# A two-layer attention kernel: layer 1's weights prepared later, and a new order of the first projection

## The chip, the cores and the metric

The kernel runs on one core of a Trainium2 chip. The metric is the device time of one execution in microseconds (us); each figure is the median of several runs. TensorE is called PE in the rows below, VectorE DVE, ScalarE ACT, GpSimd POOL and SyncE SP.

## The reference, cut to what matters

Four images `x` of 256 channels by 64x64 (4096 positions), all float32, pass through two layers, each with a group norm in front and a residual around it:

```python
# layer 0, per image, N = 4096 positions, xn = groupnorm(x)
f = Wq @ xn + bq            # 32 x N
g = Wk @ xn + bk            # 32 x N
h = Wv @ xn + bv            # 256 x N
beta = softmax(f.T @ g, over the first position axis)
x = x + gamma * (h @ beta)
# layer 1, xn = groupnorm(x)
y = relu(bn1(w1 @ xn + b1))              # 32 x N
packed = products of all pairs of y      # 528 x N
x = x + relu(bn2(w2 @ packed + b2))      # 256 x N
```

## The kernel before

Every float32 operand of a large product is split into a float16 high part and a float16 low part, and three float16 matmuls take the place of one float32 matmul. The 4096 positions of an image are cut into 8 chunks of 512 columns. For one chunk of the normed input, ACT makes the high part `xh` (`high`, L994, two instructions), DVE makes the full float32 value `xn` (`normed`, L587, two instructions) and POOL subtracts them into `xl` (`low`, L865). `xn` has two slots, so making the value of chunk k waits until POOL has used that of k-2. PE then makes queries and keys of the chunk (`queries_keys`, L1208, six matmuls) and its values (`value_pair`, L1221, twice twelve matmuls). Both results are split again: ACT copies the high part out of PSUM (`qk_high` L1003, `value_high` L1007), DVE makes the low part (`qk_low` L608, `value_low` L612). SP spreads queries and keys of a chunk over partitions with five small DMAs (`spread`, L331 to L336); `qk_high` and `qk_low` of chunk c write a buffer that the spread of chunk c-2 must have left. For the softmax a running maximum is needed: a "piece" (`piece`, L1227) is one matmul of scores into one of two PSUM banks `tps`, and DVE reduces it (`piece_max`, L617), which frees the bank. 40 pieces are done before the first attention chunk (the list `EARLY`).

Each engine runs its own list in order, and the lists are written out by hand. The front of the kernel has these parts:

- **Loads.** SP issues eight DMAs for small weights (L311), all counted by the semaphore `w_in`, then eight chunks of image 0 and eight of image 1 (L314). ACT, DVE and PE all wait until all eight weight loads have landed.
- **Set-up.** DVE scales the weights of layer 0 in a chain of small instructions, each waiting for the one before; between them it does the statistics of image 0 (`first_stats`, L431, 16 of them, interleaved by `over_stats`). The mark `scaled_qkv` (after L521) lets PE transpose layer 0's weights (L1169, L1171). DVE then scales the weights of layer 1 (L524 to L544), PE transposes them (L1176 to L1180), ACT copies them out (L967 to L973), and DVE makes their low parts (L548, L549, L566 to L569). Only after that come PE's group means (L1199), `variance` (L470 to L474), POOL's power (L858) and `bias` (L478), which give the norm its scale; ACT's first `high` waits for that.
- **Projection of image 0** (`project` on PE, ACT and DVE). ACT and DVE norm four chunks ahead (`RING` = 4); DVE then does seven small instructions of layer 1's scales (L594 to L600), for which ACT waits. After that all three engines follow the list `PARTS`, with the number of pieces after each part in `PIECES`.
- **Attention of image 0** (`attend(0)`): 8 chunks J of 32 steps t. A step is one score matmul (L1243), eight matmuls with the exponential's high part (L1377, L1378), one piece (L1227) and four with its low part (L1384) on PE; two exponentials on ACT (L1017, L1018); one reduction (L617) and one subtraction (L636) on DVE. From image 1 on, layer 1 of the image before runs between the steps. All pieces from here on use the bank `tps[0]`; `tps[1]` serves everything else.

Of the kernel before, what the change touches and what calls it, by code (L numbers as in the profile page):

```python
# [14 lines left out]
MID = 32  # L15
# [31 lines left out]
def build(nc, x, wq, wk, wv, w1, w2, vec, ident, gmean, sel, out):  # L47
# [5 lines left out]
    with ctx:  # L53
# [65 lines left out]
        wqn, wkn, w1n = ot[:, 0], ot[:, 1], ot[:, 2]  # L119
# [28 lines left out]
        w_in = sem("w_in")  # L148
# [53 lines left out]
        NLOADS = 8  # L202
# [28 lines left out]
        JOB = {job: i for i, job in enumerate(JOBS)}  # L231

# [43 lines left out]
        def rows_of(grp):  # L276
            return P if grp < 4 else 96


        PARTS = (("qk", 0), ("qk", 1), ("qk", 2), ("qk", 3), ("v", 0, 0), ("arrived", 0), ("v", 0, 1), ("v", 1, 0),  # L280
# [3 lines left out]
        PIECES = {("arrived", 0): 2, ("v", 0, 1): 2, ("v", 1, 0): 2, ("v", 1, 1): 2, ("qk", 4): 2, ("v", 2, 0): 2,  # L284
# [23 lines left out]
        def _(sp):  # L308
            for dst, src in ((vs[:], vec), (wqn, wq), (wkn, wk), (wvn, wv), (w1n, w1), (w2n, w2), (idn[:], ident),
                             (gm[:], gmean)):  # L310
                sp.dma_start(dst, src).then_inc(w_in, 16)  # L311

# [3 lines left out]
            def pass_through(kind, b, c):  # L316
                k = VISIT[kind, b, c]
                if k:
                    last = THROUGH[k - 1]
                    if last[0] == "stats":  # L320
                        sp.wait_ge(xt_free, (last[1] - 1) * NCH + last[2] + 1)
                    else:
                        sp.wait_ge(xh_ok, JOB[last] + 1)
                        sp.wait_ge(xn_ok, JOB[last] + 1)
                sp.dma_start(xt[:], xv[b, :, :, c * CH:(c + 1) * CH]).then_inc(xt_in, 16)
# [81 lines left out]
        def _(dve):  # L407
# [95 lines left out]
            dve.wait_ge(set_pool, 3)  # L503
# [20 lines left out]
            over_stats(V.tensor_reduce(col(K_MX, 2), w2n, AX, ALU.max, apply_absolute_value=True))  # L524
            over_stats(V.tensor_scalar(col(K_MX, 2), col(K_MX, 2), TINY, 2.0 ** -14, ALU.add, ALU.mult))
            over_stats(V.reciprocal(col(K_U, 2), col(K_MX, 2)))
            for h in range(H2):
                over_stats(V.tensor_scalar(w2n[:, h], w2n[:, h], col(K_U + h), None, ALU.mult))
            over_stats(V.tensor_reduce(col(K_RS1), w1n, AX, ALU.add, apply_absolute_value=True))
            over_stats(V.tensor_tensor(col(K_INV1), vc(V_G1), col(K_W), ALU.mult))  # L530
            over_stats(V.tensor_tensor(col(K_YB), col(K_RS1), col(K_INV1), ALU.mult))
            over_stats(V.tensor_scalar(col(K_RS1), col(K_RS1), TINY, 2.0 ** -7, ALU.add, ALU.mult))
            over_stats(V.reciprocal(col(K_U), col(K_RS1)))
            over_stats(V.tensor_scalar(w1n, w1n, col(K_U), None, ALU.mult))
            mark["scaled"] = s.n

            over_stats(V.tensor_tensor(col(K_T1), vc(V_B1), vc(V_M1), ALU.subtract))
            over_stats(V.scalar_tensor_tensor(col(K_T1), col(K_T1), col(K_INV1), vc(V_BE1), ALU.mult, ALU.add))

            magnitude(col(K_T), col(K_YB), 0.0, over_stats)  # L540
            over_stats(V.tensor_scalar(col(K_YB), col(K_T), GN_MAX, None, ALU.mult))
            magnitude(col(K_U), col(K_T1), 1e-15, over_stats)
            over_stats(V.tensor_tensor(col(K_YB), col(K_YB), col(K_U), ALU.add))
            over_stats(V.tensor_tensor(col(K_YB), col(K_YB), col(K_YB), ALU.mult))  # L544
            mark["squares"] = s.n

            dve.wait_ge(set_act, 1)
            V.tensor_tensor(wqkT[:, 1], acc[0][:, 0:256].rearrange("p (h c) -> p h c", h=2), wqkT[:, 0], ALU.subtract)  # L548
            over_stats(V.tensor_tensor(wvT[:, 1], acc[2][:].rearrange("p (h c) -> p h c", h=2), wvT[:, 0], ALU.subtract))  # L549
            mark["weights_qkv"] = s.n  # L550
# [3 lines left out]
            dve.wait_ge(set_pe, 4)  # L554
            over_stats(V.tensor_scalar(col(K_T), tps[1][:, 8:9], 1.0 / F16_TOP, None, ALU.mult))
            over_stats(V.reciprocal(col(K_A2), col(K_T)))
            mark["square"] = s.n

            over_stats(V.tensor_tensor(col(K_INV2, 2), vc(V_G2, 2), col(K_W + 1, 2), ALU.mult))
            over_stats(V.tensor_tensor(t2[:], vc(V_B2, 2), vc(V_M2, 2), ALU.subtract))  # L560
            over_stats(V.tensor_tensor(t2[:], t2[:], col(K_INV2, 2), ALU.mult))
            over_stats(V.tensor_tensor(t2[:], t2[:], vc(V_BE2, 2), ALU.add))
            over_stats(V.tensor_tensor(col(K_INV2, 2), col(K_INV2, 2), col(K_MX, 2), ALU.mult))

            dve.wait_ge(set_act, 2)
            V.tensor_tensor(w1T[:, 1], acc[3][:, 0:256].rearrange("p (h c) -> p h c", h=2), w1T[:, 0], ALU.subtract)  # L566
            V.tensor_tensor(w2T[:, 1, 0:2], sps[0][:].rearrange("p (g c) -> p g c", g=2), w2T[:, 0, 0:2], ALU.subtract)
            V.tensor_tensor(w2T[:, 1, 2:4], sps[1][:].rearrange("p (g c) -> p g c", g=2), w2T[:, 0, 2:4], ALU.subtract)
            s(V.tensor_tensor(w2r[32:64, :], tps[0][32:64, 0:C], w2r[32:64, :], ALU.subtract))  # L569
            mark["weights"] = s.n  # L570
            variance(0, 0)
            bias(0, 0)
            dve.wait_ge(gn_ok, 1)

# [15 lines left out]

            for c in range(RING):
                normed(("first", 0, c))
            dve.wait_ge(set_pool, 4)
            s(V.tensor_scalar(col(K_AA), col(K_AA), LO ** 0.5, None, ALU.mult))  # L594
            s(V.tensor_tensor(col(K_T), col(K_AA), col(K_AA), ALU.mult))
            s(V.reciprocal(col(K_IA), col(K_T)))
            s(V.tensor_scalar(sc2[:], col(K_INV2, 2), col(K_IA), LO, ALU.mult, ALU.mult))
            s(V.tensor_tensor(col(K_T), col(K_INV1), col(K_RS1), ALU.mult))
            s(V.tensor_tensor(s1a[:], col(K_T), col(K_AA), ALU.mult))
            s(V.tensor_tensor(t1a[:], col(K_T1), col(K_AA), ALU.mult))  # L600
            mark["scales"] = s.n
# [103 lines left out]
            def project():  # L705
                early = iter([(t, c, i % 2) for i, (t, c) in enumerate(EARLY)])
                for part in PARTS:
                    if part[0] == "qk":
                        qk_low(0, part[1], sps[part[1] % 2])
                    if part[0] == "v":  # L710
                        c, k = part[1:]
                        value_low(0, 2 * c + k, c * QT + 2 * k, h_bank(c, k))
                        if k and c + RING < NCH:
                            normed(("first", 0, c + RING))
                    if part[0] == "max":
                        tile_max(0)
                    for _ in range(PIECES.get(part, 0)):
                        piece_max(*next(early))

# [24 lines left out]
            def attend(b):  # L744
                if b == 0:
                    low_part(0)
                for J in range(NCH):
# [3 lines left out]
                    for t in range(NT):  # L751
# [7 lines left out]
                        if t + 1 < NT or J + 1 < NCH:  # L759
                            low_part(u + 1)  # L760
                        if b and n >= 1 and t in (3, 4, 7, 10, 12):
                            product_low(n - 1, (3, 4, 7, 10, 12).index(t))
# [32 lines left out]
            project()  # L795
            attend(0)
# [40 lines left out]
        def _(pool):  # L837
# [11 lines left out]
            pool.wait_ge(set_dve, mark["variances"])  # L849
            tt(sc[:, K_W:K_W + 3], sc[:, K_W:K_W + 3], exps[:, 0:3], ALU.pow).then_inc(set_pool, 1)  # L850
            pool.wait_ge(set_dve, mark["ratio"])
            tt(sc[:, K_A:K_A + 1], sc[:, K_T:K_T + 1], exps[:, 3:4], ALU.pow).then_inc(set_pool, 1)
            pool.wait_ge(set_dve, mark["square"])
# [688 lines left out]
```

## Time and profile before

| what | value |
|---|---|
| median of 3 runs | 2320.86 us (2319.19 to 2322.71) |
| the profiled execution | 2320.98 us, its span 2319.2 us (1.8 us lie around the span) |
| mean granted PE clock | 0.989 of full |
| busy: PE, DVE, ACT, POOL | 96%, 81%, 72%, 27% of the span |
| first `high` on ACT | 40.30 us after the span's start |
| first exponential on ACT (attention of image 0 begins) | 109.17 us |

A row of the timeline gives start, length, engine, source line, operation, what it writes and reads, and in square brackets how long the engine had stood idle and what released it. "SPq" is SP's DMA issue. A granted clock of 1.00 is PE's level of 2.4 GHz, 0.50 that of 1.2 GHz.

### The profile page before, as it was taken

What the parts mean: (1) busy time and instruction counts of PE and PEld (TensorE: products, weight loads), DVE (VectorE), ACT (ScalarE), POOL (GpSimd) and SP (SyncE); (2) the same over time, 40 slices, a digit from 0 to 9 for tenths busy, and PEclk for the clock granted to TensorE, in tenths of its full rate; (3) what the DMA queues carried; (4) which work ended last, traced back from release to release, by engine and by line L of the source; (5) the groups of instructions that cost most, each with busy time, mean ns of one, the idle gap of its engine ahead of it and who ended that gap; (6) DMA issues with size and microseconds to landing.
All of it is one profiled execution on the core that took longest, in us unless ns stands there. A gap on an engine that the chain in (4) does not pass through costs nothing.

```text
span 2319.2 us, 42587 instructions
## 1 busy us (share of the span) xinstructions
PE 2229.5 (96%) x16782; PEld 1638.0 (71%) x16782; DVE 1884.9 (81%) x3133; ACT 1672.2 (72%) x2691; POOL 634.9 (27%) x608
## 2 busy tenths in 40 slices
PE   2899999999999999999999999999999999999977
PEld 1577777777777777777777777777777777777722
DVE  6878888888888888888888888888888887777576
ACT  3477777777677777778777777777777777777755
POOL 2100111112222332233522133333422222222244
PEclk8999999999999999999999999999999999999979
DMA  4000000000012222220222221222101111111101
GB/s 174 24 1 1 3 6 8 8 17 1 10 52 60 70 67 54 58 59 27 56 58 68 61 65 43 54 66 57 38 26 36 30 33 33 33 33 29 33 32 55
DMA packets 56664, 95.22 MB, mean 41 GB/s; under 512 B 8016, under 2 KB 14864, under 8 KB 56464
## 3 DMA queue, kind: packets, MB, share of 16 engines
q1 hardware_dynamic: 56464, 92.49, 14.1%
q8 instruction: 133, 2.18, 0.4%
q14 instruction: 67, 0.55, 0.1%
HBM read 67.03 MB, written 19.14 MB: 37 GB/s over the span
## 4 chain that ended last, share of the span: by engine, by line
PE 91%; DVE 5%; ACT 1%; issue 1%; DMA 0%; SPq 0%; POOL 0%; POOLq 0%; DVEq 0%; ACTq 0%
PE acc L1384 19%; PE acc L1377 19%; PE acc L1378 19%; PE tps L1227 9%; PE sps L1243 9%; PE tps L1279 3%; PE acc L1221 3%; PE tps L1265 2%; PE tps L1281 2%; PE tps L1208 1%; PE acc L1279 1%; PE tps L1258 1%; DVE mx L617 1%; PE acc L1281 1%; DVE pl L636 1%
## 5 line engine op out<-in xcount | busy, mean ns | idle before, releaser
L1017 ACT ACTIVATE ph<-sps,esc 128x512 f16<-128x512 f32 x1024 | 703.7, 687 | 396.0 <-PE sps L1243 390.2
L1377 PE MATMUL acc<-hth,ph 128*128 128x257 f16 x4096 | 954.8, 273 | 3.2 <-ACT ot L1023 3.2
L1378 PE MATMUL acc<-htl,ph 128*128 128x256 f16 x4096 | 954.0, 273 | 0.0
L617 DVE TENSOR_REDUCE mx<-tps 128x1 f32<-128x512 f32 x1024 | 700.6, 686 | 300.9 <-PE tps L1227 296.6
L636 DVE TENSOR_TENSOR pl<-p,ph 128x512 f16<-128x512 f32 x1024 | 807.3, 789 | 39.2 <-ACT p L1018 38.2
L1018 ACT ACTIVATE p<-sps,esc 128x512 f32<-128x512 f32 x1024 | 700.1, 684 | 0.0
L1384 PE MATMUL acc<-hth,pl 128*128 128x257 f16 x4096 | 619.7, 273 | 0.0
L1384 PEld LDWEIGHTS acc<-hth,pl 128*128 128x128 f16 x4096 | 399.7, 98 | 159.0
L1378 PEld LDWEIGHTS acc<-htl,ph 128*128 128x128 f16 x4096 | 400.8, 98 | 150.4
L865 POOL TENSOR_TENSOR xl<-xn,xh 128x512 f16<-128x512 f32 x176 | 230.3, 1330 | 877.6 <-DVE xn L587 874.1
L1377 PEld LDWEIGHTS acc<-hth,ph 128*128 128x128 f16 x4096 | 401.0, 98 | 73.6 <-issue 4.6
L1227 PE MATMUL tps<-fst,gst 96*128 96x512 f16 x1024 | 390.4, 382 | 11.7 <-DVE mx L617 9.6
L1243 PE MATMUL sps<-gst,fst 128*128 128x512 f16 x1024 | 388.4, 379 | 1.2 <-ACT p L1018 1.2
L897 POOL TENSOR_TENSOR rt<-rt,yb 128x512 f32<-128x512 f32 (+1 forms) x120 | 183.5, 1560 | 15.3 <-DMA rt<-turned 15.3
L888 POOL TENSOR_TENSOR r<-nm,mw 128x4 f32<-128x4 f32 x32 | 18.1, 567 | 465.6 <-DVE nm L632 465.6
L1227 PEld LDWEIGHTS tps<-fst,gst 96*128 96x128 f16 x1024 | 100.1, 98 | 39.2 <-DVE mx L617 22.0
L1243 PEld LDWEIGHTS sps<-gst,fst 128*128 128x128 f16 x1024 | 100.4, 98 | 28.5 <-issue 1.7
L1279 PE MATMUL tps<-qh,w2T 128*128 128x512 f16 x368 | 109.5, 379 | 0.0
L994 ACT ACTIVATE xh<-xb,nbias,rstd 128x512 f16<-128x512 f32 x136 | 102.5, 809 | 8.3 <-DVE nbias L478 4.5
L903 POOL TENSOR_TENSOR zt<-zt,xb 128x512 f32<-128x512 f32 x48 | 64.8, 1351 | 137.3 <-ACT zt L1056 137.3
L1044 ACT ACTIVATE qh<-rt 128x512 f16<-128x512 f32 (+1 forms) x140 | 87.3, 627 | 15.2 <-DVE rt L683 15.2
L699 DVE SCALAR_TENSOR_TENSOR ql<-qh,rt 128x512 f16<-128x512 f16 x112 | 79.0, 706 | 4.0 <-ACT qh L1044 4.0
(212 smaller groups left out, 1633.4 us busy)
## 6 DMA issues: line engine op xcount, KB each, us to landing
rt<-turned SPq DMA_DIRECT2D x96, 256.0 KB, 4.3
xt<-x SPq DMA_DIRECT2D x36, 512.0 KB, 3.8
xb<-x SPq DMA_DIRECT2D x32, 512.0 KB, 5.0
out<-zt SPq DMA_DIRECT2D x48, 256.0 KB, 2.1
rt<-turned SPq DMA_DIRECT2D x72, 64.0 KB, 4.8
turned<-yb SPq DMA_DIRECT2D x24, 96.0 KB, 1.9
out<-fst SPq DMA_DIRECT2D x8, 256.0 KB, 2.0
out<-htl SPq DMA_DIRECT2D x8, 256.0 KB, 2.0
```

Source lines behind the costliest of these rows:

```text
L617: V.reduce_max(mx[:, tile, c:c + 1], tps[par][:], AX).then_inc(t_free[par], 1)
L636: V.tensor_tensor(pl[:, u % SLOTS], p32[:, u % SLOTS], ph[:, u % SLOTS], ALU.subtract).then_inc(pl_ok, 1)
L865: last = tt(xl[:, k % RING, h], xn[:, k % 2, h], xh[:, k % RING, h], ALU.subtract)
L897: tt(rt0[0:rows, grp], rt0[0:rows, grp], yb0[0:rows, :], ALU.mult).then_inc(pb_ok, 1)
L1017: A(ph[:, u % SLOTS], sps[u % 2][:], ACT.Exp, scale=esc[:]).then_inc(ph_ok, 1)
L1018: A(p32[:, u % SLOTS], sps[u % 2][:], ACT.Exp, scale=esc[:]).then_inc(p32_ok, 1)
L1227: fill(mm(tps[par][:], gst[0:96, key_tile(b * NT + tile)], fst[0:96, b % 2, c * CH:(c + 1) * CH], start=True, stop=True), par)
L1243: mm(sps[u % 2][:], fst[:, G // NCH % 2, tile * P:(tile + 1) * P], gst[:, keys_at(G)], start=True, stop=True).then_inc(s_mm, 1)
L1279: mm(bank[:], w2T[:, w, grp, cols], qh[k][:, grp], start=(grp == 0 and w == 0), stop=False)
L1377: mm(acc[j][:, 0:C + 1], w, hth[:, t], start=(t == 0), stop=False)
L1378: mm(acc[j][:, 0:C], w, htl[:, t], start=False, stop=False)
L1384: last = mm(acc[j][:, 0:C + 1], pl[:, u % SLOTS, j * P:(j + 1) * P], hth[:, t], start=False, stop=(t == NT - 1))
```

## The change

The weights of layer 1 are no longer made in the set-up. Their DVE work becomes a generator `second_weights`, of which one piece is done at each of 29 listed steps of the attention of image 0 (J = 0 to 2); PE's twelve transposes follow at steps (1, 18), (1, 21) and (2, 9), ACT's copies two steps later, with the bank `tps[1]`. The two POOL powers that belong to them move between POOL's `value_bias` calls. The six weight loads that stay in `w_in` are issued by ACT; SP starts with image 0 and loads `w1` and `w2` behind it. A row of constants that ACT wrote twice is copied by one DMA the second time. In the projection ACT makes both the high part and the float32 value of chunks 2 to 7 (`BY_ACT`); DVE makes the value of chunks 0 and 1 alone. `PARTS` and `PIECES` are gone: three short loops give a new order.

```diff
-            for dst, src in ((vs[:], vec), (wqn, wq), (wkn, wk), (wvn, wv), (w1n, w1), (w2n, w2), (idn[:], ident),
-                             (gm[:], gmean)):
-                sp.dma_start(dst, src).then_inc(w_in, 16)
...
             for c in range(NCH):
                 load(0, c)
+            sp.dma_start(w1n, w1).then_inc(w1_in, 16)
+            sp.dma_start(w2n, w2).then_inc(w1_in, 16)
+            sp.wait_ge(fc_ok, 1)
+            sp.dma_start(fst[96:P, 1], fst[96:P, 0]).then_inc(fc_in, 16)
             for c in range(NCH):
                 load(1, c)
@@ vector: set-up @@
-            s(V.tensor_scalar(col(K_W), vc(V_V1), BN_EPS, None, ALU.add))
-            s(V.tensor_scalar(col(K_W + 1, 2), vc(V_V2, 2), BN_EPS, None, ALU.add))
-            mark["variances"] = s.n
-            s(V.tensor_copy(idh[:], idn[:]))
...
             mark["scaled_qkv"] = s.n
-            (the chains of layer 1, L524 to L545, come out here)
             while counted[0] < H2 * NCH:
                 first_stats()
             moments(0, 0)
+            dve.wait_ge(set_act, 1)
+            V.tensor_tensor(wqkT[:, 1], ...)
+            V.tensor_tensor(wvT[:, 1], ...).then_inc(set_dve, 1)
             variance(0, 0)
             bias(0, 0)
             dve.wait_ge(gn_ok, 1)
+            def second_weights():   # the same operations, with a yield after each one or two
...
+            SECOND = [(0, t) for t in range(27, 32)] + [(1, t) for t in range(10, 18)]
+            SECOND += [(1, t) for t in (18, 19, 20, 21, 22, 23, 25, 27)] + [(2, t) for t in (10, 13, 14, 16, 26, 28, 29, 30)]
@@ vector: project @@
+                for c in range(2):
+                    normed(("first", 0, c))
+                s(V.tensor_copy(idh[:], idn[:]))
+                for c in range(NCH):
+                    qk_low(0, c, sps[c % 2])
+                    if c >= 2:
+                        pieces(QT)
+                    if c:
+                        for k in range(2):
+                            value_low(0, 2 * c - 2 + k, QT * c - QT + 2 * k, h_bank(c - 1, k))
+                pieces(QT)
+                for k in range(2):
+                    value_low(0, 2 * NCH - 2 + k, NT - QT + 2 * k, h_bank(NCH - 1, k))
+                pieces(QT)
+                tile_max(0)
+                pieces(NCH)
@@ scalar: set-up, high, project @@
+            for dst, src in ((vs[:], vec), (wqn, wq), (wkn, wk), (idn[:], ident), (gm[:], gmean), (wvn, wv)):
+                act.dma_start(dst, src).then_inc(w_in, 16)
...
-            A(fst[96:P, 1], gst[96:P, 0:HW], ACT.Identity, bias=vs[96:P, V_FROW:V_FROW + 1])
...
+                if job in BY_ACT:
+                    act.wait_ge(xl_ok, k - 1)
+                    for h in range(H2):
+                        last = A(xn[:, k % 2, h], xb[0][:, h, c * CH:(c + 1) * CH], ACT.Identity,
+                                 bias=nbias[0][:, h:h + 1], scale=rstd[0][:, h:h + 1])
+                    last.then_inc(xa_ok, 1)
...
+                for c in range(3):
+                    high(("first", 0, c))
+                qk_high(0, 0, sps[0])
+                high(("first", 0, 3))
+                for c in range(1, NCH):
+                    qk_high(0, c, sps[c % 2])
+                    for k in range(2):
+                        value_high(0, 2 * c - 2 + k, QT * c - QT + 2 * k, h_bank(c - 1, k))
+                    if c + 3 < NCH:
+                        high(("first", 0, c + 3))
+                for k in range(2):
+                    value_high(0, 2 * NCH - 2 + k, NT - QT + 2 * k, h_bank(NCH - 1, k))
                 row_copy(0, sps[0])
@@ tensor: project, attend @@
+                for c in range(NCH):
+                    if c >= 2:
+                        pe.wait_ge(qk_lo, c - 1)
+                    queries_keys(("first", 0, c), sps[c % 2])
+                    if c >= 2:
+                        pieces(QT)
+                    if c:
+                        pair_of_values(c - 1)
+                pieces(QT)
+                pair_of_values(NCH - 1)
+                pieces(QT + 5)
...
+                rows(0, sps[0])
+                pieces(3)
...
+                        if b == 0 and (J, t) in ((1, 18), (1, 21), (2, 9)):
+                            free(1)
+                            second_weights(((1, 18), (1, 21), (2, 9)).index((J, t)))
```

## Rows read from the trace of the kernel before

**Rows 1.** Page: busy us (share of the span) and instructions of each engine.
```profile
PE 2229.5 (96%) x16782; PEld 1638.0 (71%) x16782; DVE 1884.9 (81%) x3133; ACT 1672.2 (72%) x2691; POOL 634.9 (27%) x608
```
**Rows 2.** Windows: stretch, length, busy (count) PE PEld DVE ACT POOL, PEclk, DMA, GB/s.
```profile
62.00:109.17 47.17, 38.29 (x236) 22.81 (x236) 40.93 (x71) 17.75 (x29) 11.44 (x15) 0.96 0.09 24
```
**Rows 3.** DMA of 0 to 112 us: GB/s in 40 slices; size, us to landing.
```profile
GB/s 42 237 314 356 405 393 387 386 386 388 212 0 0 0 0 0 0 0 0 47 62 67 59 53 0 0 59 12 25 45 0 60 13 29 47 0 3 0 0 0
zt<-wv SPq DMA_DIRECT2D x1, 256.0 KB, 2.8
gm<-gmean SPq DMA_DIRECT2D x1, 64.0 KB, 5.3
```
**Rows 4.** Timelines of SP and DVE: the loads, the set-up and the norm.
```profile
4.47 15.94 SPq L314 DMA_DIRECT2D xb<-x  x16
...
9.34 0.15 DVE L485 TENSOR_SCALAR sc<-vs 128x1 f32<-128x1 f32 x1 [5.83 <-DMA gm<-gmean]
9.99 0.42 DVE L490 TENSOR_REDUCE sc<-ot 128x1 f32<-128x256 f32 x1
25.66 0.17 DVE L521 TENSOR_SCALAR mw<-mw 128x4 f32<-128x4 f32 x1
25.86 1.42 DVE L524 TENSOR_REDUCE sc<-rt 128x2 f32<-128x1216 f32 x1
32.61 0.68 DVE L549 TENSOR_TENSOR wvT<-acc,wvT 128x512 f16<-128x512 f32 x1
38.48 0.16 DVE L470 COPY gsb<-tps 128x4 f32<-128x4 f32 x1 [0.77 <-PE tps L1199]
```
**Rows 5.** Timeline of ACT: copies in the set-up, then the first norms.
```profile
27.74 0.59 ACT L964 ACTIVATE wvT<-acc 128x512 f16<-128x512 f32 x1
40.30 5.75 ACT L994 ACTIVATE xh<-xb,nbias,rstd 128x512 f16<-128x512 f32 x8 [3.81 <-issue]
```
**Rows 6.** Timelines of the three engines: one round of the projection (chunk 5 to 6).
```profile
78.69 0.69 ACT L1003 ACTIVATE zt<-sps,bqk 128x512 f16<-128x512 f32 x1 [0.45 <-PE sps L1208]
83.00 0.60 ACT L1007 ACTIVATE hth<-acc 128x512 f16<-128x512 f32 x1 [0.93 <-PE acc L1221]
83.49 1.50 ACT L994 ACTIVATE xh<-xb,nbias,rstd 128x512 f16<-128x512 f32 x2
85.17 0.69 ACT L1003 ACTIVATE qkh<-sps,bqk 128x512 f16<-128x512 f32 x1 [0.17 <-PE sps L1208]
79.59 0.74 DVE L608 SCALAR_TENSOR_TENSOR zt<-sps,bqk,zt 128x512 f16<-128x512 f32 x1
80.25 1.27 DVE L617 TENSOR_REDUCE mx<-tps 128x1 f32<-128x512 f32 x2
```
**Rows 7.** The chain that ended last: start, length, what; twelve matmuls at either clock.
```profile
64.66 2.57 PE acc L1221 x12
80.12 1.31 PE acc L1221 x12
```
**Rows 8.** Windows of 2 us in the projection (columns as in Rows 2).
```profile
62.00:64.00 2.00, 0.39 (x1) 0.10 (x1) 2.00 (x5) 1.80 (x3) 0.00 (x0) 1.00 0.24 61
64.00:66.00 2.00, 1.95 (x9) 1.25 (x10) 2.00 (x4) 0.00 (x0) 0.35 (x1) 0.50 0.26 65
66.00:68.00 2.00, 2.00 (x12) 1.27 (x11) 0.81 (x3) 0.60 (x1) 1.91 (x2) 0.65 0.09 25
100.00:102.00 2.00, 0.56 (x2) 0.10 (x1) 1.61 (x3) 0.36 (x1) 0.00 (x0) 1.00 0.00 0
```
**Rows 9.** Timeline of PE in the attention: steps without and with four transposes.
```profile
173.28 0.38 PE L1243 MATMUL sps<-gst,fst 128*128 128x512 f16 x1
175.04 0.38 PE L1243 MATMUL sps<-gst,fst 128*128 128x512 f16 x1
175.25 0.60 PE L1258 MATMUL tps<-idn,ot 128*128 128x128 f32 x4
177.23 0.38 PE L1243 MATMUL sps<-gst,fst 128*128 128x512 f16 x1
```

More of the change, by code:

```diff
@@ L231, in build @@
         JOB = {job: i for i, job in enumerate(JOBS)}
+        BY_ACT = [("first", 0, c) for c in range(2, NCH)]
+        BY_DVE = {job: sum(j not in BY_ACT for j in JOBS[:i + 1]) for i, job in enumerate(JOBS)}
         THROUGH = []
@@ L706, in project, with pieces @@
                 early = iter([(t, c, i % 2) for i, (t, c) in enumerate(EARLY)])
[L707 to L717, printed above, removed]
-                        piece_max(*next(early))
+                def pieces(count):
+                    for _ in range(count):
+                        piece_max(*next(early))
+                for c in range(2):
+                    normed(("first", 0, c))
+                s(V.tensor_copy(idh[:], idn[:]))
+                mark["half"] = s.n
+                for c in range(NCH):
[11 more added lines that the diff above has]
+                pieces(NCH)
             def values(b):
@@ L760, in attend @@
                             low_part(u + 1)
+                        if b == 0 and (J, t) in SECOND:
+                            next(weights)
                         if b and n >= 1 and t in (3, 4, 7, 10, 12):
@@ L795, in _ @@
             project()
+            weights = second_weights()
             attend(0)
@@ L1115, in _ @@
             act.wait_ge(set_dve, mark["scaled_qkv"])
-            for c in range(RING):
-                high(("first", 0, c))
-            act.wait_ge(set_dve, mark["scales"])
             project()
             attend(0)
+            act.wait_ge(set_dve, mark["scales"])
             for b in range(1, B):
@@ L1295, in project, with pieces, pair_of_values @@
                 early = iter([(t, c, i % 2) for i, (t, c) in enumerate(EARLY)])
-                for part in PARTS:
-                    if part[0] == "qk":
-                        if part[1] >= 2:
-                            pe.wait_ge(qk_lo, part[1] - 1)
-                        queries_keys(("first", 0, part[1]), sps[part[1] % 2])
-                    if part[0] == "v":
-                        c, k = part[1:]
+                def pieces(count):
+                    for _ in range(count):
+                        tile, c, par = next(early)
+                        if tile == 0:
+                            pe.wait_ge(fg_in[c % 2], spreads(0, c))
+                        piece(0, tile, c, par)
+                def pair_of_values(c):
+                    for k in range(2):
                         if c >= 2:
@@ L1305, in project @@
                         value_pair(("first", 0, c), k, h_bank(c, k))
-                    if part[0] == "arrived":
-                        pe.wait_ge(fg_in[0], spreads(0, 0))
-                    if part == ("v", 1, 0):
-                        pe.wait_ge(fg_in[1], spreads(0, 1))
-                    if part[0] == "rows":
-                        pe.wait_ge(qk_lo, NCH)
-                        rows(0, sps[0])
-                    for _ in range(PIECES.get(part, 0)):
-                        tile, c, par = next(early)
-                        if tile == 0 and c >= 2:
-                            pe.wait_ge(fg_in[c % 2], spreads(0, c))
-                        piece(0, tile, c, par)
+                for c in range(NCH):
[9 more added lines that the diff above has]
+                pieces(QT + 5)
+                pe.wait_ge(qk_lo, NCH)
+                pe.wait_ge(set_dve, mark["half"])
+                rows(0, sps[0])
+                pieces(3)
                 pe.wait_ge(m_ok, 1)
@@ L1321, in project, with second_weights @@
                 pe.wait_ge(h_lo, 2 * NCH)
+            def second_weights(part):
+                pe.wait_ge(set_dve, mark[("scaled", "part0", "part1")[part]])
+                for i in range(H2):
+                    at = slice(i * P, (i + 1) * P)
+                    if part == 0:
+                        tr(tps[1][:, at], w1n[:, at], idn[:])
+                        last = tr(tps[1][0:96, C + i * P:C + (i + 1) * P], w2n[:, i, 4 * P:W2C], idn[:])
+                    else:
+                        for g in range(2):
+                            grp = 2 * part - 2 + g
+                            last = tr(tps[1][:, g * C + i * P:g * C + (i + 1) * P], w2n[:, i, grp * P:(grp + 1) * P],
+                                      idn[:])
+                last.then_inc(set_pe, 1)
             def rest_of_z(n):
@@ L1388, in attend @@
                         last.then_inc(p_free, 1)
+                        if b == 0 and (J, t) in ((1, 18), (1, 21), (2, 9)):
+                            free(1)
+                            second_weights(((1, 18), (1, 21), (2, 9)).index((J, t)))
+                        if b == 0 and (J, t) == (2, 13):
+                            pe.wait_ge(set_dve, mark["weights"])
+                            mm(tps[1][:, 8:9], ones[0:MID, :], sc[0:MID, K_YB:K_YB + 1], start=True,
+                               stop=True).then_inc(set_pe, 1)
                         if b and nxt and t == 9:
@@ L1413, in attend @@
                                 pe.wait_ge(y_ok, n + 1)
+                            else:
+                                pe.wait_ge(set_dve, mark["read"])
                             moments(first_norm(b + 1), 0, 1)
```

227 lines of the change are left out of this document (130 added, 97 removed), and 6 rows, old and new, of tables (PARTS, PIECES).

## The prediction

> **What bounds the kernel now.** The page's first table gives TensorE 96% of the span and VectorE 81% [rows 1]; that is an average over the whole kernel. The attention is bound by TensorE: a step starts 1.755 us after the one before (173.28 to 175.04), and nothing lies between [rows 9]. What the change rebuilds is the front, which ends with the first exponential at 109.17 us. I read it in order of time. (1) Loads: VectorE starts when the last of eight weight loads lands, at 9.34. (2) Set-up: from 9.99 to 25.83 VectorE does layer 0's chain with the statistics between, then layer 1's weights; the norm's scale comes after all of it, and ScalarE's first `high` starts at 40.30 [rows 4, 5]. (3) Projection, 68.9 us: in 62 to 109.17 VectorE is busy 40.9 of 47.2 us, TensorE 38.3, ScalarE 17.8 only [rows 2]. So ScalarE looks free there. But look at how a round is chained [rows 6]: queries and keys copied by ScalarE at 78.69, low part by VectorE at 79.59, two reductions, pieces and values on TensorE, a copy of values at 83.00, the next chunk's `high` (1.50), and only then the next copy of queries and keys, 6.48 us after the first. What is put on ScalarE between the value copy and that copy lengthens the round, however idle ScalarE is on average.
>
> **Part 1, the weight loads.** Eight loads (1.39 MB by their sizes) become six (0.65 MB) on ScalarE's queue, with image 0 issued beside them. The trace shows no ScalarE issue; I take SP's 0.43 to 0.47 each [rows 4], so the last is issued at about 3.1. Lower bound: undisturbed it lands 2.8 later, as wv did, at 5.9. Upper bound: it lands behind all of image 0 that was issued before, about 2.1 MB in all; at 42, 237, 314 and 356 GB/s in slices of 2.8 us [rows 3] that is 9.3, no gain. In between, if both queues share evenly, 1.3 MB have moved when the weights are in: 0.78 by 5.6 us, the rest at 314 GB/s, 7.3. I take 7.3. Image 0 moves 3.75 us earlier in SP's list (16 loads took 15.9 us to issue) and its chunks arrive ahead of the statistics that read them.
> The Trainium skill (DMA: Bandwidth & Descriptors, "Issuing engines are not separate DMA queues") says that DMAs of all issuing engines run on the same 16 engines and interleave, so that a second issuer saves its issue time alone. This speaks against a large gain here; by it 7.3 or later is the value, and no run shown here has two issuers.
>
> **Part 2, the set-up.** Three small instructions (9.34 to 9.99) leave the path. Layer 0's chain stays: 15.84 us (9.99 to 25.83) [rows 4]. Then, in the new order: transposes and ScalarE's copies end 2.50 after `scaled_qkv` (28.33 less 25.83); `moments` fits beneath that; two subtractions, 0.68 and half of it, 1.03 with gaps; `variance` to the first `high` as before, 38.48 to 40.30, 1.82 [rows 4, 5]. Together 5.35 in place of 14.47. First `high`: 7.3 + 15.84 + 5.35 = **28.5**, 11.8 us earlier. With the bounds of part 1, 27.1 to 30.5. The constant row becomes a DMA for which SP waits ahead of image 1's loads; even with 10 us of waiting after the weights, those eight loads (1.0 each) are issued by 26, and the first spread is wanted near 35: nothing.
>
> **Part 3, the projection.** ScalarE's pair costs 1.42 spaced (5.75 for eight) [rows 5]; for chunks 2 to 7 there are now two pairs. VectorE loses six pairs and the seven scale instructions, but that helps only where it is last. Up to the third query copy ScalarE is the path: eight pairs in all (chunks 0 to 4 high, chunks 2 to 4 float32) 11.4, two query copies 1.2, two value copies with their wait 1.1: 13.6.
> A round with a `high` is then: query copy 0.69, low part 0.67, two reductions 1.28, release and one piece 0.28, two times twelve matmuls 2.62 [rows 7] with 0.2 to drain, the last value copy 0.49, two pairs 2.84 [rows 5, 6]; with about 0.04 at the hand-overs, **9.1 us**, against 6.48 to 7.1 before. There are three such rounds (copy 2 to copy 5): 27.3. The two rounds without a `high` take TensorE's next query group instead, 1.3 with drain 0.17: 7.05 each, 14.1. From the eighth query copy to the first exponential: values of chunk 6 (5.6), pieces and values of chunk 7 (5.6), copies and four maxima (3.9), the row maximum through GpSimd, TensorE and ScalarE and two scores (4.7): 19.8. Sum 13.6 + 27.3 + 14.1 + 19.8 = **74.8**, if TensorE ran at full clock all along; before it took 68.9. That puts the first exponential at 103.3, 5.9 us early.
> But it will not keep its clock. In a round of 9.1 us TensorE works 4.8; between its second piece and its fourth, some 4.8 us together, it has 0.4 us of work. In the kernel before, a stretch like that (62 to 64, 0.39 busy) was followed by a granted clock of 0.50 from 64 on, and it was back at 1.00 only after some 3.4 us of dense work (66 to 68 still mixed) [rows 8]. While it is at 1.2 GHz a group of twelve matmuls takes 2.57 in place of 1.31 [rows 7]: 1.26 more, and in the new round the two value groups are on the path. So I charge each of the seven rounds one to two groups, taking 1.3 on average (11.5), and one group at the cold start (1.3): **13** more, about 88 in all. Ends: no group, 74.8; two groups in each round and in the tail, 94.
> The Trainium skill (TensorE: Matmul & The Clock Gate, "Part 1: The HAM clock gate") calls the throttled level the default that activity releases; the rows above agree, 0.50 after the idle stretch. By that rule alone a more gapped projection costs more than its matmul count tells.
> First exponential: 28.5 + 88 = 116.5, **7.3 us later** than 109.17.
>
> **Part 4, layer 1's weights inside the attention.** On TensorE, four transposes lengthen a step from 1.755 to 2.19 [rows 9], so twelve cost 1.3, and one tiny matmul 0.1, all on the bounding engine. VectorE's work (most of what lay between 25.83 and 37.7, the reduction of 1.42 now in two) goes to 29 steps; a step leaves it some 0.5 us idle, and steps such as (1, 11), (1, 12) and (1, 20) to (1, 23) get 0.4 to 0.8 on top of statistics of 0.6. The next piece waits when a reduction is more than 0.65 late. I count 0.8 for that, ends 0 and 4. ScalarE's five copies and two scalings fit into its gaps. Sum **+2.2**, ends 1.4 and 5.4. GpSimd's two powers wait for VectorE at places where it has nothing due.
>
> **The sum.** 2320.98 (the profiled run, which lies 0.12 above the median) + 7.3 + 2.2 = **2330.5 us**, +0.41%. About 0.2%, 4.6 us, is what a measurement of this kernel can tell from no change.
>
> **Rivals.** (a) *TensorE keeps its full clock through the projection*; then 103.3 + 2.2 against 109.17, -3.7: 2317.3. For it: 100 to 102 had 0.56 busy and stayed at 1.00 [rows 8]. Against it: that gap stood between dense stretches, the new ones are twice as long and come every round. It decides below three half-rate groups: break-even is a projection of 78.5 us, 3.7 above 74.8. Chance 0.12. (b) *ScalarE's extra pairs do not lie in the round*: the next query copy goes as early as before and a round stays at 6.5 to 7.1. Then the three rounds give back 7, nothing goes cold, and the time is about 2310.5. It would need the list's order to matter less than the chain says. Chance 0.10. (c) *The clock stays low for most of the projection, or VectorE's extras stall the attention at their upper end*: 94 in place of 88 and +5.4: about 2339. Chance 0.08. The forecast has 0.70, its own range 2325 to 2336.
>
> **The numbers.** Range 2316 to 2336: up to the forecast's end, down through (a). Faster by over 0.2% (below 2316.2): (b) and a little of (a), 0.13. Within 0.2%: most of (a) and the low edge of the forecast, 0.16. Slower: 0.71.
>
> **What would show it.** In the profile after: the last weight DMA landing near 7.3; the first `high` at 28.5 (right if within 2); the spacing of ScalarE's query copies in chunks 2 to 5, 9 to 12 us against 6.5 to 7.1, with four `xh`/`xn` instructions directly ahead of each; granted clock of 0.50 recurring after 40 us; the first exponential near 116; the steps (1, 18), (1, 21), (2, 9) 0.44 longer. The prediction is wrong if the clock stays at 1.00, if the rounds are near 7, or if the set-up is much shorter than the chain of 21 us after the loads.

## The result, and the profile after

The changed kernel takes 2339.58 us (median of 4 runs, 2338.49 to 2341.7) against 2321.02 for the kernel before in the same comparison: ratio 1.008, 95% interval 1.0064 to 1.0096. It is slower, as forecast, but by 18.6 us where 9.5 were forecast. The profiled execution has a span of 2337.6 us against 2319.2, 18.4 more; all that follows divides these 18.4.

The set-up, as DMAs, VectorE and ScalarE show it (the answer to [rows 3 to 5]). First the sizes and landing times of the DMAs issued in the first 12 us, then rows of the three timelines:

```profile
xb<-x SPq DMA_DIRECT2D x8, 512.0 KB, 8.8
zt<-wv ACTq DMA_DIRECT2D x1, 256.0 KB, 7.6
gm<-gmean ACTq DMA_DIRECT2D x1, 64.0 KB, 6.7
```

```profile
0.72 4.94 SPq L304 DMA_DIRECT2D xb<-x  x8
...
3.48 0.48 ACTq L1006 DMA_DIRECT2D zt<-wv  x1
...
11.13 0.42 DVE L480 TENSOR_REDUCE sc<-ot 128x1 f32<-128x256 f32 x1 [7.62 <-DMA zt<-wv]
...
26.88 0.17 DVE L511 TENSOR_SCALAR mw<-mw 128x4 f32<-128x4 f32 x1
...
30.53 0.15 DVE L464 COPY gsb<-tps 128x4 f32<-128x4 f32 x1
...
32.34 4.34 ACT L1045 ACTIVATE xh<-xb,nbias,rstd 128x512 f16<-128x512 f32 x6 [2.78 <-issue]
```

VectorE waits for wv until 11.13, 1.8 us later than it waited before, though two loads fewer stand in the way. From there the set-up runs as forecast: 15.92 us for layer 0's chain (15.84 in the sum), 5.29 more to the first `high` (5.35), which starts at 32.34.

One round of the projection, ScalarE's and VectorE's timeline (the answer to [rows 6]):

```profile
58.92 0.67 ACT L1060 ACTIVATE zt<-sps,bqk 128x512 f16<-128x512 f32 x1
64.73 0.60 ACT L1064 ACTIVATE hth<-acc 128x512 f16<-128x512 f32 x1 [5.15 <-PE acc L1275]
66.34 0.60 ACT L1064 ACTIVATE hth<-acc 128x512 f16<-128x512 f32 x1 [1.00 <-PE acc L1275]
66.83 1.51 ACT L1045 ACTIVATE xh<-xb,nbias,rstd 128x512 f16<-128x512 f32 x2
68.24 1.51 ACT L1051 ACTIVATE xn<-xb,nbias,rstd 128x512 f32<-128x512 f32 x2
69.65 0.67 ACT L1060 ACTIVATE qkh<-sps,bqk 128x512 f16<-128x512 f32 x1
```

```profile
59.62 0.75 DVE L639 SCALAR_TENSOR_TENSOR zt<-sps,bqk,zt 128x512 f16<-128x512 f32 x1 [2.69 <-ACT zt L1060]
60.29 2.58 DVE L648 TENSOR_REDUCE mx<-tps 128x1 f32<-128x512 f32 x4
```

ScalarE waits 5.15 us for the first values and 1.00 for the second, and is then busy without a gap, with the second copy of values and two pairs, until the next copy of queries and keys. That makes 10.73 us from copy to copy (58.92 to 69.65), against 6.48 before. TensorE's clock in windows of 2 us (columns as in [rows 2]; the answer to [rows 8]):

```profile
68.00:70.00 2.00, 0.03 (x1) 0.00 (x0) 0.00 (x0) 2.00 (x4) 0.11 (x1) 1.00 0.00 0
70.00:72.00 2.00, 0.24 (x1) 0.10 (x1) 1.64 (x3) 0.32 (x1) 2.00 (x2) 1.00 0.14 33
72.00:74.00 2.00, 1.81 (x8) 1.08 (x8) 1.59 (x3) 0.00 (x0) 0.15 (x1) 0.50 0.22 56
```

After 68 to 72 with 0.27 us of work the granted clock is 0.50. The mean from 62.00 to the first exponential is 0.79 against 0.96 before. The projection of the kernel before also had a half-clock part, at its start, so over the whole projection the means are closer, 0.82 against 0.88. The first exponential starts at 119.98, 87.6 us after the first `high`.

The attention of image 0. GpSimd's first instruction for each row maximum (from the second row below on it comes near step 24 of a chunk) marks its progress; in the kernel before, the same marks lie at 103.04, 153.56, 211.88, 270.32, 330.35:

```profile
114.69 0.20 POOL L930 TENSOR_TENSOR r<-nm,mw 128x4 f32<-128x4 f32 x1 [31.99 <-DVE nm L663]
166.91 0.57 POOL L930 TENSOR_TENSOR r<-nm,mw 128x4 f32<-128x4 f32 x1 [49.54 <-DVE nm L663]
228.13 0.58 POOL L930 TENSOR_TENSOR r<-nm,mw 128x4 f32<-128x4 f32 x1 [50.80 <-DVE nm L663]
286.84 0.58 POOL L930 TENSOR_TENSOR r<-nm,mw 128x4 f32<-128x4 f32 x1 [1.99 <-DVE nm L663]
348.48 0.58 POOL L930 TENSOR_TENSOR r<-nm,mw 128x4 f32<-128x4 f32 x1 [13.21 <-DVE nm L663]
```

The delay is 13.35 at the second mark, 16.25, 16.52 and 18.13 at the next three, and it stays at 18.13 through the next four. It is 18.31 from 650 us on and 18.77 from 1110 us on to the last mark (2129.33 before, 2148.10 after), and the stretch behind the last mark is 0.4 shorter. So all but 0.3 us net of the loss lies ahead of 302 us. It divides so:

| stretch | forecast | measured |
|---|---|---|
| first `high` | -11.8 | -7.96 (32.34 against 40.30) |
| first `high` to first exponential | +19.1 (88 against 68.9) | +18.8 (87.64 against 68.87) |
| first three steps of the attention | 0 | +2.5 |
| layer 1's weights in the attention | +2.2 | +4.8 |
| rest | 0 | +0.3 |
| sum | +9.5 | +18.4 |

### The profile page after: what moved, and what is told of

It is laid out like the page before. It is cut to its first block, busy times and chain, and to the rows that moved or that the text cites. A ratio compares the mean times of both kernels' runs of the same rounds, so it can differ in the third digit from the quotient of the medians.

```text
span 2337.6 us, 42608 instructions
## 1 busy us (share of the span) xinstructions
PE 2240.0 (96%) x16782; PEld 1642.1 (70%) x16782; DVE 1875.9 (80%) x3122; ACT 1676.5 (72%) x2702; POOL 634.1 (27%) x608
## 4 chain that ended last, share of the span: by engine, by line
PE 91%; DVE 5%; ACT 2%; issue 1%; POOL 0%; DMA 0%; POOLq 0%; ACTq 0%; DVEq 0%
PE acc L1460 19%; PE acc L1453 19%; PE acc L1454 18%; PE tps L1281 9%; PE sps L1297 9%; PE acc L1275 4%; PE tps L1333 3%; PE tps L1319 2%; PE tps L1335 2%; DVE mx L648 1%; PE tps L1262 1%; PE acc L1333 1%; PE tps L1312 1%; DVE pl L667 1%; ACT xh L1045 1%
## 5 line engine op out<-in xcount | busy, mean ns | idle before, releaser
L1275 PE MATMUL acc<-wvT,xh 128*128 128x256 f16 x464 | 86.2, 292 | 0.0
```

## The experiments

Eight kernels ran. "First high", "projection" (to the first exponential) and the marks are of each one's profiled execution; the kernel before has 40.30, 68.9 and a span of 2319.2. The eight ran in two groups, on different chips. The first (e1, e2, e3, e5) has a median of 2321.55 for the kernel before, the second (e4, e7, e8, e10) one of 2326.22, so medians are compared within a group, or as ratios to the kernel before.

Spans need care as well. The stretch behind the last mark, which no edit of these runs touches, took 188.8 to 194.0 us in the profiled executions, with the dips of the granted clock at different places, so single spans differ by up to 5 us for that alone. What an edit is worth is therefore read at the last mark, against the kernel before (2129.33) in the first row and against the changed kernel (2148.10) in the second:

| | changed | e1 | e2 | e3 | e4 | e5 | e7 | e8 | e10 |
|---|---|---|---|---|---|---|---|---|---|
| last mark, against before | +18.8 | +12.2 | -1.0 | +6.1 | +9.8 | -6.8 | -12.6 | -13.3 | +15.5 |
| last mark, against changed | 0 | -6.6 | -19.8 | -12.7 | -9.0 | -25.6 | -31.3 | -32.0 | -3.3 |
| behind the last mark | 189.5 | 189.4 | 194.0 | 188.8 | 193.5 | 190.0 | 189.9 | 190.0 | 192.3 |

**e1_loads_sp: the weights on SP's queue ahead of the image.**

```diff
-            for dst, src in ((vs[:], vec), (wqn, wq), (wkn, wk), (idn[:], ident), (gm[:], gmean), (wvn, wv)):
-                act.dma_start(dst, src).then_inc(w_in, 16)
... (the line above is in ScalarE's list, the lines below are in SP's)
+            for dst, src in ((vs[:], vec), (wqn, wq), (wkn, wk), (wvn, wv), (idn[:], ident), (gm[:], gmean)):
+                sp.dma_start(dst, src).then_inc(w_in, 16)
             for c in range(NCH):
                 load(0, c)
```

> The changed kernel with its six small weight loads issued by SP ahead of image 0, as before the change, and none by ScalarE. Theory A (image 0's chunks, issued beside the weights, hold the weights up: the last landed at 11.13 us): the last weight lands near 7, the first high starts near 28 in place of 32.34, the rest is unchanged, total near 2335.5. Rival B (the queue of issue does not matter; six loads need that long on any queue): landing near 11, total near 2339.6.

Measured 2335.04 us, ratio to before 1.0055 (1.004 to 1.007); the last weight lands at 6.42 and the first `high` starts at 27.72, 4.6 us earlier; projection 85.8. Span 2330.9, 6.7 less than the changed kernel's; 4.6 are the loads and 1.9 a shorter projection (the granted clock differs in places, 0.97 in place of 0.83 from 90 to 100 us; no run isolates why). Theory A holds.

**e10_x_waits: the weights on ScalarE's queue, the image held back.**

```diff
+            sp.wait_ge(w_in, 16 * NLOADS)
             for c in range(NCH):
                 load(0, c)
```

> The changed kernel, weights on ScalarE's queue as it has them, but SP issues image 0 only when all six weights have landed. Theory A (image 0's traffic holds them up): the last weight lands at 6 to 7 us in place of 11.13, and the first high starts near 28 to 29 in place of 32.34. Rival B (ScalarE's queue is slow by itself): the last weight lands at 10 or later.

DMA list and VectorE's timeline of this run:

```profile
zt<-wv ACTq DMA_DIRECT2D x1, 256.0 KB, 2.8
```

```profile
5.92 0.42 DVE L481 TENSOR_REDUCE sc<-ot 128x1 f32<-128x256 f32 x1 [2.41 <-DMA zt<-wv]
...
9.63 0.69 DVE L426 BATCH_NORM_STATS2 bst<-xb 128x6 f32<-128x512 f32 x1 [0.89 <-DMA xb<-x]
```

On the same queue, with no traffic of the image beside it, wv lands 2.8 us after its issue in place of 7.6. ScalarE's queue is not slow; the image's traffic holds the weights up. The statistics then wait 0.9 us for the image, and the first `high` starts at 28.12, as theory A said. This kernel was executed once. It took 2338.85 us, with a projection of 88.6, 1 us longer than the changed kernel's; that single total settles nothing, and at the last mark it is 3.3 us ahead.

**e2_act_order: only ScalarE's list reordered.**

```diff
                 for c in range(1, NCH):
                     qk_high(0, c, sps[c % 2])
+                    if c >= 2 and c + 2 < NCH:
+                        high(("first", 0, c + 2))
                     for k in range(2):
                         value_high(0, 2 * c - 2 + k, QT * c - QT + 2 * k, h_bank(c - 1, k))
-                    if c + 3 < NCH:
-                        high(("first", 0, c + 3))
```

> The changed kernel with ScalarE's list alone reordered: the norm pairs of a later chunk stand directly behind the copy of queries and keys (where ScalarE stands idle for over 5 us of each round) in place of directly ahead of the next one. Same instructions, same number. Theory A (the float32 pairs lengthen the round because of where they stand): rounds near 7 to 8 us in place of 8.7 to 11.3, first high to first exponential 70 to 79 us in place of 87.6, total near 2325. Rival B (ScalarE's place does not matter, TensorE's order and clock do): 87 us, total near 2339.

```profile
59.45 0.69 ACT L1060 ACTIVATE qkh<-sps,bqk 128x512 f16<-128x512 f32 x1 [0.70 <-PE sps L1262]
60.04 1.51 ACT L1045 ACTIVATE xh<-xb,nbias,rstd 128x512 f16<-128x512 f32 x2
61.45 1.50 ACT L1051 ACTIVATE xn<-xb,nbias,rstd 128x512 f32<-128x512 f32 x2
63.91 0.60 ACT L1064 ACTIVATE hth<-acc 128x512 f16<-128x512 f32 x1 [0.96 <-PE acc L1275]
65.22 0.60 ACT L1064 ACTIVATE hth<-acc 128x512 f16<-128x512 f32 x1 [0.71 <-PE acc L1275]
66.52 0.69 ACT L1060 ACTIVATE zt<-sps,bqk 128x512 f16<-128x512 f32 x1 [0.70 <-PE sps L1262]
```

In ScalarE's timeline the same two pairs now fill the wait for values, and the round is 7.07 us. The last five rounds are all 7.06 to 7.07; the granted clock reads 1.00 from 42 to 94 us, without a further edit. Projection 69.2 us in place of 87.6 (theory A's range was 70 to 79); 2326.17 us, ratio 1.0014 (1.0005 to 1.0023). With the same instructions it is some 15 us faster by the two ratios (1.0014 against 1.008), and 19.8 ahead at the last mark: most of the projection's loss comes from the place of the pairs, not from their number.

The repair is not complete. In the last stretch ahead of the attention TensorE still has gaps, and the clock falls there:

```profile
90.00:100.00 10.00, 7.37 (x34) 3.10 (x31) 7.64 (x15) 1.79 (x3) 2.35 (x7) 0.77 0.00 0
100.00:110.00 10.00, 8.73 (x50) 5.37 (x50) 6.36 (x11) 6.23 (x11) 0.00 (x0) 0.72 0.01 2
```

In windows of 2 us it is 1.00 until 94 us, after one with 0.44 us of work in it, and 0.50 from 96 to 104 us, which is past the first exponential (101.45). So the stretch from the first exponential to the second mark takes 45.73 us in place of 44.39 before the change.

**e3_keep_clock: TensorE kept busy in its idle stretches.**

```diff
                     if c >= 2:
-                        pieces(QT)
+                        pieces(2)
+                        if c >= 3:
+                            pe.wait_ge(h_lo, 2 * (c - 3) + 1)
+                        extra(h_bank(c - 1, 0), 12)     # 12 matmuls of 512 columns, result unread
+                        pieces(2)
...
-                pieces(QT + 5)
+                pe.wait_ge(h_lo, 2 * NCH - 3)
+                for _ in range(QT + 5):
+                    pieces(1)
+                    extra(acc[0], 1)                    # and one behind each of the last 12 pieces
```

> The changed kernel with extra matmuls on TensorE whose result nobody reads: twelve of 512 columns between the second and the third piece of each round, where TensorE stands idle, and one after each of the last twelve pieces. Theory A (part of the loss is the half clock after the idle stretches): granted clock near 1.00 from the second round on, projection 76 to 81 us in place of 87.6 and no slow first steps of the attention (2.8 us), total near 2327. Rival B (the clock is low but off the path, the round is set by ScalarE): rounds and total unchanged, 2339 or more.

```profile
57.02 0.67 ACT L1060 ACTIVATE zt<-sps,bqk 128x512 f16<-128x512 f32 x1
61.46 0.60 ACT L1064 ACTIVATE hth<-acc 128x512 f16<-128x512 f32 x1 [3.77 <-PE acc L1275]
62.77 0.60 ACT L1064 ACTIVATE hth<-acc 128x512 f16<-128x512 f32 x1 [0.71 <-PE acc L1275]
63.27 1.51 ACT L1045 ACTIVATE xh<-xb,nbias,rstd 128x512 f16<-128x512 f32 x2
64.68 1.50 ACT L1051 ACTIVATE xn<-xb,nbias,rstd 128x512 f32<-128x512 f32 x2
66.09 0.67 ACT L1060 ACTIVATE qkh<-sps,bqk 128x512 f16<-128x512 f32 x1
```

With the granted clock at 1.00 from 40 us to the attention, ScalarE's rounds with two pairs are 9.07 us (57.02 to 66.09), the 9.1 that the prediction's sum gave for full clock; projection 77.3 us (the sum: 74.8, and 1.3 for the cold start). From the first exponential to the second mark it takes 44.39 us, exactly as before the change (109.17 to 153.56), where the changed kernel takes 46.93. 2327.48 us, ratio 1.0021 (1.0011 to 1.003): matmuls that do nothing put the changed kernel 12.7 us ahead at the last mark. So the half clock costs the changed projection 10.3 us (87.6 less 77.3), or more if the added matmuls cost time themselves, and the 2.5 us at the attention's start are its work too.

**e4_xn_dve: the new order, VectorE makes all float32 values.**

```diff
-        BY_ACT = [("first", 0, c) for c in range(2, NCH)]
+        BY_ACT = []
...
-                for c in range(2):
+                for c in range(3):
                     normed(("first", 0, c))
...
                     qk_low(0, c, sps[c % 2])
+                    if c == 0:
+                        normed(("first", 0, 3))
...
                         for k in range(2):
                             value_low(0, 2 * c - 2 + k, QT * c - QT + 2 * k, h_bank(c - 1, k))
+                        if c + 3 < NCH:
+                            normed(("first", 0, c + 3))
```

> The changed kernel with its new order, but every float32 value made by VectorE again (chunks 0 to 2 ahead, 3 behind the first low part, 4 to 7 behind the two low parts of values in each round); ScalarE keeps one pair per chunk. Theory A (a round is lengthened by what stands on ScalarE ahead of the next copy, 1.42 us for one pair, and then by the half clock): first high to first exponential 75 to 84 us in place of 87.6, total near 2330. Rival B (the new order itself is the loss, whoever makes the values): 85 us or more, total near 2338.

Projection 75.6 us; rounds of 7.66, 9.32, 7.66 and 8.72 (copies at 46.22, 53.88, 63.20, 70.86, 79.58); 2330.71 us, ratio 1.0021 (1.0012 to 1.003). One pair fewer in each round, and about two thirds of the projection's loss is gone, as theory A said; the clock still falls in places (0.83 in 70 to 80), and so the rounds differ. The profiled execution was the longest of the ten (2334.38), with 193.5 us behind the last mark.

**e5_old_order: the old order of the projection, the rest as changed.** `PARTS`, `PIECES` and the three `project` functions of the kernel before are put back, with `BY_ACT = []`; the moved weights and the loads on ScalarE's queue stay.

> The changed kernel with the projection's old order on all three engines (the old parts and pieces) and all float32 values made by VectorE again; the moved weights, the loads on ScalarE's queue and the new set-up stay. Theory A (the projection's new order and ScalarE's part are the main loss): first high at 32.3, projection 65 to 68 us, attention as in the changed kernel without its slow first steps (+4.8 against before), total near 2317. Rival C (the weights inside the attention are the main loss): total above 2330.

Projection 64.2 us; 2315.06 us, ratio **0.9975** (0.9965 to 0.9984), span 2312.5. From the first exponential to the second mark 44.4 us, as before. Theory A, with the projection 0.8 us below its range. The moved weights, with the loads as the change has them, gain 6.5 us; the new order and ScalarE's share turn that into a loss of 18.6.

The projection is here 4.7 us shorter than in the kernel before, with the same order of parts on each engine. One difference is plain in the timelines: before its first copy of queries and keys ScalarE waited 6.35 us for layer 1's scale instructions in the kernel before, and it waits 1.14 us here. So the new order is to be measured against this run: next to 64.2 us the changed projection loses 23.5 us, and not 18.8.

**e7_loads_old_order: as the last, with e1's loads.**

> The old order of the projection with VectorE's float32 values, and the six weight loads on SP ahead of image 0; the moved weights stay. If the gains of the two repairs add up: first high near 27.8, projection 64 us, total near 2310.5. If the projection then waits for something else (image 0 lands later, spreads): 2313 to 2315.

First `high` at 27.39, projection 63.5 us, and 5.8 us ahead of e5 at the last mark: the two repairs add up. 2314.54 us, ratio **0.9954** (0.9938 to 0.9971) against e5's 0.9975. As a number 2314.54 lies in the range that was named for a projection that waits for something else (2313 to 2315), but the projection did not wait, and the kernel before is 4.7 us slower in this group. The totals alone do not separate e7 from e5: their intervals overlap.

**e8_slots: as the last, with layer 1's pieces at other steps.**

```diff
-            SECOND = [(0, t) for t in range(27, 32)] + [(1, t) for t in range(10, 18)]
-            SECOND += [(1, t) for t in (18, 19, 20, 21, 22, 23, 25, 27)] + [(2, t) for t in (10, 13, 14, 16, 26, 28, 29, 30)]
+            SECOND = [(0, t) for t in range(27, 32)] + [(1, t) for t in (1, 2, 3, 4, 7, 10, 13, 14)]
+            SECOND += [(1, t) for t in (17, 18, 20, 21, 22, 23, 25, 27)] + [(2, t) for t in (10, 13, 14, 16)]
+            SECOND += [(3, t) for t in (10, 11, 12, 13)]
```

> As the run before with the 29 pieces of layer 1's weights at other steps of the attention of image 0: eight of them at steps of J = 1 without statistics (1, 2, 3, 4, 7, 10, 13, 14), the last four at (3, 10) to (3, 13) in place of (2, 26), (2, 28), (2, 29), (2, 30). Theory A (3 of the 4.8 us that the attention lost are VectorE coming late where statistics, norms and these pieces meet; 1.3 are transposes and 0.4 the tiny matmul): the attention's part falls to about 2, total 2.7 below the run before, near 2308. Rival B (the loss is TensorE's own added work): no more than 1 us of difference.

Marks two to five of this run and of the one before it, from GpSimd's timelines: 137.46, 197.71, 256.43, 316.47 against 135.23, 196.80, 255.52, 317.14. Chunk 1 took 60.25 in place of 61.57 us and the stretch from the fourth mark to the fifth 60.04 in place of 61.62 (before the change 58.32 and 60.03): 2.9 us less, as theory A says. At the last mark only 0.7 us of it is left, since the first `high` came 0.2 later, the projection took 0.3 longer, and in this profiled execution the clock dipped once at 90 to 100 us (0.83), so that the first chunk took 1.7 us longer. 2311.06 us, ratio **0.9935** (0.992 to 0.995). That is the lowest median here, 3.5 us below e7's, but with four runs each the intervals overlap; the gain is shown for the two stretches and not for the total. At the last mark it is 32.0 us ahead of the changed kernel.

## Why the prediction came out as it did

The measured loss is 8.9 us larger than the forecast, and three terms make it up: the loads 3.8, the first steps of the attention 2.5, the moved weights 2.6. The projection was 0.3 below its forecast and the rest 0.3 above.

**Right: what ends the projection.** The round was to be set by what ScalarE does ahead of the next copy of queries and keys, 9.1 us at full clock; e3 measured 9.07, and e2, which moves those pairs alone, 7.07 for a round that the sum gave as 7.05 without them. The projection was forecast at 88 us and took 87.6. That the two agree so closely is partly luck: without the half clock it took 77.3 us where the sum gave 76.1 (74.8 and the cold start), and the half clock took 10.3 where 11.5 was charged, so two misses of 1.2 cancel.

**Right: the clock.** The charge for groups of matmuls at 1.2 GHz is confirmed in kind by e3, which removes the half clock and 10.3 us with it. Rival (a), a clock that stays full, is refuted by the trace, and rival (b), pairs that do not lie in the round, by e2 and e3. Rival (c) named 2339, close to the measured 2339.58, but by a projection of 94 us that did not come. The stated range ended at 2336, although the parts' own upper ends (2.0 us for the set-up, 6 for the projection, 3.2 for the attention) reach 2341.7 together.

**Wrong: Part 1, the weight loads.** The step that failed is the traffic ahead of the weights: the landing at 7.3 assumed that both queues share evenly, and the upper bound 9.3 that "about 2.1 MB in all" stand ahead. (At the rates it quotes, 2.1 MB take 9.6 us.) The 2.1 MB come from 1.0 us of issue per chunk, which is 15.9 us for 16 issues. That mean hides two rates: an issue takes 0.43 to 2.28 us in the kernel before, and the changed kernel's first eight take 4.94 together. When wv was issued at 3.48, SP had issued four chunks and was on its fifth; by 11.13 SP's queue had moved 2.63 MB, which is five chunks, and ScalarE's 0.67 MB, 3.30 MB in all (only 0.28 and 0.01 MB of it before 3.3 us). That is no even share, and it is about what had been issued before wv or beside it, where I had counted under three chunks. Which packets went first inside the queues is not shown. The landing, and with it the first `high`, came 3.8 us later than forecast and beyond the upper bound. e10 and e1 name the cause from both sides: wv lands at 5.92 on the same queue without the image, and the first `high` starts at 27.7 with the weights in front. The Trainium skill's rule that a second issuing engine gives no bandwidth of its own (DMA: Bandwidth & Descriptors, "Issuing engines are not separate DMA queues") was the rule that spoke against the edit. The trace agrees: from 3.1 to 11.13 us the two queues together moved 350 to 414 GB/s, and before the change SP's alone moved 336 to 414 from 9 to 28 us. The prediction priced this too kindly.

**Wrong: Part 4, the attention.** +2.2 was the sum, its upper end 5.4; measured are 4.8 for the moved weights, inside the ends, and 2.5 that no term held, 7.3 together. Step by step, from the starts of TensorE's score matmuls in both traces:

- Transposes at (1, 18), (1, 21), (2, 9): 0.44 each, 1.3, as forecast.
- The tiny float32 matmul: 0.42 in place of 0.1. It lies alone between two steps, from 267.99 until the next score matmul starts at 268.30, which was due at 267.89 by the spacing of the steps around it.
- VectorE late: 2.8 in place of 0.8 (the ends were 0 and 4). 1.6 of it lies in one place, (2, 30), for which the prediction named no price:

```profile
293.78 2.72 POOL L907 TENSOR_TENSOR xl<-xn,xh 128x512 f16<-128x512 f32 x2 [4.90 <-DVE xn L630]
294.15 1.33 DVE L667 TENSOR_TENSOR pl<-p,ph 128x512 f16<-128x512 f32 x1
295.41 1.10 DVE L603 TENSOR_TENSOR sc<-sc 128x1 f32<-128x1 f32 x1
296.49 1.36 POOL L919 TENSOR_SCALAR xb<-xb,gbv 128x512 f32<-128x512 f32 x2
296.55 0.16 DVE L604 RECIPROCAL sc<-sc 128x1 f32<-128x1 f32 x1
296.75 0.69 DVE L648 TENSOR_REDUCE mx<-tps 128x1 f32<-128x512 f32 x1
297.35 1.03 DVE L667 TENSOR_TENSOR pl<-p,ph 128x512 f16<-128x512 f32 x1
297.50 0.39 PE L1281 MATMUL tps<-fst,gst 96*128 96x512 f16 x1 [1.23 <-DVE mx L648]
```

These are rows of the three timelines of the changed kernel around step (2, 30). A multiplication of one column took 1.10 us while GpSimd ran `xl`; it ends at 296.51, `xl` at 296.50. The piece of scores behind it waited 1.23 for VectorE. The subtraction next to it took 1.33 in place of its usual 0.68, but that is not the change's work: before it, the same subtraction beside `xl` took as long. In e8 the same multiplication, which stands there at 292.44 with GpSimd idle, took 0.15. The subtraction in the kernel before:

```profile
277.26 2.72 POOL L865 TENSOR_TENSOR xl<-xn,xh 128x512 f16<-128x512 f32 x2 [4.90 <-DVE xn L587]
277.63 1.33 DVE L636 TENSOR_TENSOR pl<-p,ph 128x512 f16<-128x512 f32 x1
```

I had counted steps with statistics only. e8 moved these pieces and got 1.6 back there, and 1.3 in chunk 1.
- The first three steps of the attention run at half clock: 2.5. The prediction followed the clock to the first exponential and stopped. Windows of the changed kernel from 114 to 126 us show 0.50 throughout, as in this one; e3 removes it.

```profile
124.00:126.00 2.00, 2.00 (x10) 1.26 (x9) 1.29 (x2) 0.56 (x1) 0.00 (x0) 0.50 0.00 0
```

- 0.2 at (1, 1), of unsettled cause.

**Open.** That GpSimd's work is what stretches VectorE's instructions at (2, 30) is read from the overlap (1.10 beside it, 0.15 without); no run changed GpSimd's work alone. Which of the new order and the float32 share loses how much is not one number. Against the old order in e5 (64.2) they lose 23.5 us together, the new order with the pairs in e2's place loses 5.0, and the new order without ScalarE's float32 share (e4) 11.4. Why the clock dips at other places behind the last mark from one execution to the next is not shown either.

## What to carry to other kernels

An engine that is 38% busy can still set a round: ask what stands in its list directly ahead of the instruction that the next engine waits for, and put movable work behind it, into the wait. When a round grows, add what the half clock will cost, and follow it past the place where the edit ends. When two versions are compared by single executions, compare them at a mark behind the edit, since a stretch that no edit touches can differ by 5 us. Before splitting loads over two queues, compare with the bytes of the bulk transfer that will be in flight; small urgent loads belong in front of it.

## What the runs showed of the hardware

- A 256 KB load took 2.8 us to land behind five smaller loads of its own queue (e10), and 7.6 us where another queue moved 2.6 MB by the time it landed, at 350 to 414 GB/s in all from 3.1 us on.
- Twelve matmuls of 512 columns in each round, whose result nobody reads, together with one behind each of the last twelve pieces, kept the granted clock at 1.00 and took 10 us off a projection in which it otherwise fell to 0.50 in most rounds.
- A float32 matmul of one column (32x1) took 0.42 us out of TensorE's full-clock stream, as much as four 128x128 transposes (0.44).
- A VectorE multiplication of one column took 1.10 us beside a GpSimd subtraction of 128x512 and 0.15 with GpSimd idle.
